# First layer's loop: TensorE's registers of adjacency slots and blocks are loaded one by one behind adjacency products, a pair of groups ahead

## What is computed

```python
# first layer, per edge
scores = jnp.sum(Q[tgt] * K[src], axis=-1) / math.sqrt(DK)
smax = jax.ops.segment_max(scores, tgt, num_segments=n)
sexp = jnp.exp(scores - smax[tgt])
...
# second layer, twice; the kernel does this sum as a product with a dense matrix
msg = x[src] * ew[:, None]
agg = jax.ops.segment_sum(msg, dst, num_segments=n)
...
x = _layernorm(x + layer(x), axis=-1)   # around each of the four
```

## Time and profile before

| | |
|---|---|
| Timed runs, median of 3 | 6169.95 us (6169.24 to 6170.06) |
| Profiled execution, span | 8199.2 us (the page gives no other time of it) |
| The loop in the profiled execution | 207 to 1930 us |
| TensorE busy in that stretch | 1252.18 us of 1723 |
| GpSimd busy in that stretch | 817.12 us |
| VectorE busy in that stretch | 914.52 us |
| ScalarE busy in that stretch | 611.39 us |
| Granted TensorE clock in that stretch | 0.71 of full speed |

### The profile page before, as it was taken

One profiled execution on the slowest core, in us unless ns is written; L12 is line 12 of the kernel. 1 busy time (PEld: TensorE's weight loads), 2 busy tenths in 40 slices (PEclk: granted clock), 3 DMA queues, 4 the chain that ended last, 5 costly groups with the idle time before them and its releaser, 6 DMA issues. The chain is left out here.

```text
span 8199.2 us, 128493 instructions
## 1 busy us (share of the span) xinstructions
PE 5007.5 (61%) x25366; PEld 3730.4 (45%) x25375; DVE 4287.8 (52%) x10883; ACT 2730.0 (33%) x6600; POOL 3533.6 (43%) x3882
## 2 busy tenths in 40 slices
PE   2677777774888935555556345555555355655557
PEld 2555555553664524444444334444444244444443
DVE  6555555556664145555555545554556445555554
ACT  1333333333542003333334323333334133333342
POOL 2544444442320044555554445555552555555520
PEclk7676677776999965555556556555556555555568
DMA  2444444443444722222222122222221222222215
GB/s 72 128 137 135 137 134 139 134 137 86 134 134 158 249 54 58 64 62 62 65 59 61 42 54 63 62 59 66 60 63 35 54 60 61 60 60 61 58 35 202
DMA packets 579250, 728.81 MB, mean 89 GB/s; under 512 B 90091, under 2 KB 424769, under 8 KB 578686
## 3 DMA queue, kind: packets, MB, share of 16 engines
q0 software_dynamic: 123968, 282.81, 14.9%
q1 hardware_dynamic: 304800, 350.53, 14.5%
q10 hardware_dynamic: 149918, 88.82, 4.0%
HBM read 601.07 MB, written 120.75 MB: 88 GB/s over the span
## 5 line engine op out<-in xcount | busy, mean ns | idle before, releaser
L1769 POOL DMA_INDIRECT rows<-scratch_gat,index x2496 | 2437.4, 977 | 2757.1 <-DVE mix L1997 1461.9
L2103 PE MATMUL sums<-xr_part,hot_t 128*128 x7524 | 1106.9, 283 | 786.2 <-issue 466.9
L2158 PE MATMUL sums<-mix,vhot 128*128 128x128 f32 x4992 | 1261.8, 421 | 91.0 <-issue 81.7
L2103 PEld LDWEIGHTS sums<-xr_part,hot_t 128*128 128x128 bf16 x7524 | 775.5, 121 | 1102.7 <-issue 945.7
L2011 DVE TENSOR_TENSOR z<-sums,rows 128x512 f32<-128x512 f32 x624 | 428.7, 687 | 1563.0 <-remote 1425.4
L1836 ACT ACTIVATE moved_sums<-sums x624 | 373.1, 598 | 2620.8 <-remote 1599.0
L932 POOL DMA_INDIRECT rows<-scratch_kv,index_ring x832 | 820.6, 986 | 887.5 <-ACT index_ring L1242 661.3
L2158 PEld LDWEIGHTS sums<-mix,vhot 128*128 128x128 f32 x4992 | 1044.4, 303 | 186.6 <-issue 142.6
L1368 PE MATMUL sums<-at_hot,lo_hot 128*128 128x200 f32 x2496 | 820.1, 493 | 16.4 <-issue 11.2
L1826 ACT ACTIVATE vhot<-iota,edge_local 128x128 f32<-128x128 f32 x2496 | 791.2, 392 | 0.1
L2154 PE MATMUL sums<-zeros 128*128 128x8 bf16 x624 | 114.7, 184 | 999.9 <-issue 551.5
(11 more groups left out here) (514 smaller groups left out, 6385.9 us busy)
## 6 DMA issues: line engine op xcount, KB each, us to landing
piece<-scratch_adj SPq DMA_DIRECT2D x90, 1280.0 KB, 6.3
local_ring<-scratch_local_rows SPq DMA_DIRECT2D x633, 128.0 KB
scratch_spool<-rows ACTq DMA_DIRECT2D x208, 256.0 KB, 2.6
vals<-scratch_spool SPq DMA_DIRECT2D x208, 256.0 KB, 2.6
scratch_adj<-stage SPq DMA_DIRECT2D x25, 1600.0 KB
rows<-scratch_gat,index POOLq DMA_INDIRECT x2496
local_ring<-scratch_local_rows ACTq DMA_DIRECT2D x211, 128.0 KB
mask<-scratch_masks SPq DMA_DIRECT2D x234, 80.1 KB
```

The costliest lines, as they stand in the source:

```text
L1769: eng.indirect_dma_start(rows[:, slot, q, k * LINE:(k + 1) * LINE], None, table, bass.IndirectOffsetOnAxis(ap=index[:, slot, s:s + 1], axis=0)
L2103: ins = eng.matmul(B.ps[:, at + k * D:at + (k + 1) * D], hot_t[:, slot, k * P:(k + 1) * P], part[:, bass.ds(at_block, D)], start=(j == 0), ...
L2158: ins = eng.matmul(B.ps[:, bass.ds(of_block * D, D)], hot[:, v % MIXES, k * P:(k + 1) * P], mix[:, v % MIXES, k * D:(k + 1) * D], start=Fa ...
```

## The change

The two loads at the head of each even group are taken out. In their place five loads of one register each stand behind adjacency products, and fill the registers of the next pair: three from `A.pe_table` behind the first three products of an even group, two from `B.blocks` behind the first two products of an odd group. The first pair's five loads stand ahead of the loop. Both tables get a pad of zeros for the pair behind the last. The registers are no longer handed over to the values read from them (`donate` is gone). On ScalarE, the value of the wait for room is worked out in a register of its own by two register instructions.

```diff
+    def fetch(self, at, n):
+        self.eng.load([self.regs[at]], self.B.blocks[0:1, bass.ds(n * GROUP, GROUP)].bitcast(I32))
+
+    def held(self, at):
+        return self.eng.snap(self.regs[at], min_val=0, max_val=(1 << 30) - 1)
...
-        self.pe_table = B.sb(ctx, "adj_pe_table", [1, A_STEPS], mybir.dt.uint8)
-        self.evac_table = B.sb(ctx, "adj_evac_table", [1, A_STEPS // 2], u16)
+        self.pe_table = B.sb(ctx, "adj_pe_table", [1, A_STEPS + A_TURN], mybir.dt.uint8)
+        self.evac_table = B.sb(ctx, "adj_evac_table", [1, (A_STEPS + A_TURN) // 2], u16)
...
+                eng.memset(A.pe_table[:, A_STEPS:], 0)
+                eng.memset(A.evac_table[:, A_STEPS // 2:], 0)
...
-                            need = field(twos[0], NEED_FIELD.bit_length() - 1, 32, BLOCKS - 1)
-                            eng.wait_ge(room.sem, need + (room.at(0) + 1))
+                            eng.reg_alu(need, twos[0] // NEED_FIELD, 31, ALU.bitwise_and)
+                            eng.wait_ge(room.sem, eng.snap(need, min_val=0, max_val=BLOCKS - 1) + (room.at(0) + 1))
...
+
+                def load_slots(pair, h, j):
+                    eng.load([regs[h][j]], A.pe_table[0:1, bass.ds(pair * A_TURN + 4 * j, 4)].bitcast(I32))
+
+                def load_ahead(i, q, k):
+                    h = q // 2 + 1
+                    if q % 2 == 0 and k < A_TURN // 4:
+                        load_slots(i * pairs + h, h % pairs, k)
+                    if q % 2 == 1 and k < 2:
+                        blocks.fetch(2 * (h % pairs) + k, i * RING_GROUPS + 2 * h + k)
+                for j in range(A_TURN // 4):
+                    load_slots(0, 0, j)
+                for k in range(2):
+                    blocks.fetch(k, k)
                 with eng.Fori(0, RING_TURNS) as i:
                     for q in range(RING_GROUPS):
                         n = i * RING_GROUPS + q
                         if q % 2 == 0:
-                            pair = i * (RING_GROUPS // 2) + q // 2
-                            eng.load(regs[q // 2], A.pe_table[0:1, bass.ds(pair * A_TURN, A_TURN)].bitcast(I32))
-                            slots = [eng.snap(r, donate=True, min_val=0, max_val=(1 << 31) - 1) for r in regs[q // 2]]
-                            fours = blocks.load(q, 2, n)
+                            slots = [eng.snap(r, min_val=0, max_val=(1 << 31) - 1) for r in regs[q // 2]]
+                            fours = [blocks.held(q), blocks.held(q + 1)]
...
                             if k % 2:
                                 ins.then_inc(summed.sem, 1)
+                            load_ahead(i, q, k)
```

More of the change, by code:

```diff
@@ L1104, in _ @@
                 slot(tmp, bank, 1)
-                link(eng.scalar_tensor_tensor(out=A.pe_table[:, :], in0=tmp[:, 0:A_STEPS], scalar=16.0, in1=read[:, 0:A_STEPS],
+                eng.memset(A.pe_table[:, A_STEPS:], 0)
+                eng.memset(A.evac_table[:, A_STEPS // 2:], 0)
+                link(eng.scalar_tensor_tensor(out=A.pe_table[:, 0:A_STEPS], in0=tmp[:, 0:A_STEPS], scalar=16.0, in1=read[:, 0:A_STEPS],
                                               op0=ALU.mult, op1=ALU.add))
@@ L1125, in _ @@
                     scalar=float(NEED_FIELD), in1=by_turn[:, :, 0], op0=ALU.mult, op1=ALU.add))
-                link(eng.tensor_copy(A.evac_table[:, :], read[:, 0:n]))
+                link(eng.tensor_copy(A.evac_table[:, 0:n], read[:, 0:n]))
                 next_block = bounds[0:1, 0:BLOCKS * BLOCK_WINDOWS].rearrange("p (k j) -> p k j", j=BLOCK_WINDOWS)[:, 1:BLOCKS, 0]
@@ L1261, in _ @@
                 regs = [[eng.alloc_register(f"evac{B.fresh()}") for j in range(A_TURN // 4)] for h in range(pairs)]
+                need = eng.alloc_register(f"need{B.fresh()}")
                 for n in range(3):
@@ L1295, in _ @@
                         keep(n, q)
-                for r in sum(regs, []):
+                for r in sum(regs, []) + [need]:
                     eng.free_register(r)
```

## The result

| | median of the runs, us | range, us |
|---|---|---|
| before | 6170.01 | 6169.24 to 6174.74 (4 runs) |
| changed | 6296.17 | 6292.02 to 6307.68 (4 runs) |

The ratio is 1.022, with a 95% interval from 1.0197 to 1.0242: slower by 126 us, 1.21 us for each of the 104 pairs. The prediction was slower by 35 us, and its range ended at 6250.

A forecast was written before the change was run, and what follows sets the result against it. TensorE's sequencer was taken as the bound. The middle of +27 and +80 us, 53, weighted by two thirds for low-clock groups, gave +35 us, the rest 0: 6170 to 6205, range 6090 to 6250.

The forecast's parts named there:

- What bounds the kernel: In the loop of 104 pairs, TensorE waits for its sequencer; without stalls a pair would be 10.65 us.
- everybody waits for TensorE: In the loop, GpSimd waits 651 us and ScalarE 581, TensorE only 31 for `hot_t`, so TensorE sets the pace.
- Removed and added: TensorE's sequencer loses a 1.70 us block at the pair's head and gains 2.47 us: 0.77 us more a pair.
- What hides it: Loads behind adjacency products: hidden at the low clock, lead of 0.5 us at the full clock; +35 us in all.
- the two views: Extra cost at the full clock: +0.26 us a pair (+27 us) seen from matmuls, +0.77 (+80 us) from the sequencer.
- What is late next: Adjacency sums come up to 1.5 us later, but ScalarE's 5.9 us before `hot_t` stays covered by TensorE's 6.2.
- The rest: Loads ahead of the loop, VectorE's clears and ScalarE's wait value: counted as 0, with +5 us for the range.
- Another engine sets the pace: Rival: GpSimd's 10.4 or ScalarE's 9.9 us a pair decides; within 12 us of 6170; no measurable change had 0.26.
- The loads get hidden: Rival: even group's three loads hidden at the low clock, 0.72 us a pair saved, 75 us, 6095; faster had 0.28.
- The change does not do what it says: Rival: loads don't overlap matmuls at either clock; 1.26 us a pair, +131 us, 6301; above 6250 had 0.04.
- What was to show it: Changed profile: 300 ns single loads, no 1.2 us even-head idle, full-clock adjacency parts 1.0 (even), 0.5 us (odd) longer.
- GpSimd's wait for index copies: Sign in the changed profile: if this wait grows instead of staying, the prediction's sum is wrong.

The follow-up runs named there:

- old loop: Loop of the kernel before with only ScalarE's edit of the change, profiled on a chip without the 0.7 us stalls; 6164.61 us against 6167.02.
- 2: Old loop with five single loads in place of the two bulk loads, all at the even group's head, nothing loaded ahead; 6217.17 us, ratio 1.0088.
- 5: Changed kernel with ScalarE's register load issued in the odd group before, behind `hot_t`; 6213.29 us, ratio 1.0077 to before.
- 6: Kernel before with ScalarE's register load issued in the odd group before, behind `hot_t`; 6152.86 us, ratio 0.9988.
- 3: Changed kernel with bulk loads in place of single ones, each behind a group's first product, a pair ahead; 6303.36 us, ratio 1.0232 to before.
- experiment 1: Kernel before with only ScalarE's edit of the change, the wait value worked out in its own register; 6164.61 us against 6167.02, ratio 1.0.
- 9: 6 with slots and blocks in one merged table, read by one load of five registers at the even head; 6139.95 us, ratio 0.9964 to before.
- 8: Changed kernel with only the three slot loads ahead in the even group, the block registers a bulk load at the pair's head; 6182.99 us, ratio 1.0033 to before.
- experiment 7: 3 with both bulk loads behind the even group's last product, at the odd group's head; 6256.41 us, ratio 1.015 to before.

## Why the prediction was wrong

The prediction left 0.04 to a time above 6250; 6296 was measured.

**What bounds the kernel: right where it was timed, but not read rightly.** On the timed chips TensorE's sequencer is at work for 11.06 of the old loop's 11.68 us a pair, and the loss lies in the loop only. That timed runs lack the 0.7 us stops was right too. But "TensorE waits 31 us for `hot_t`" was read from a view of idle matmul time. In the same trace of before the sequencer stood at that wait for 2.92 us in each pair, 304 us in all; 104 of these waits are over 1 us, and each ends 0.04 us behind the end of a `hot_t`. So the wait that later grew stood in the rows' trace already, and "everybody waits for TensorE" was half of it.

**Removed and added: right in kind, too small.** The sum was +0.77 us of sequencer time a pair; measured is +1.01 (12.07 less 11.06). The six new instructions with what lies between them were put at 0.56 (0.14 for addresses and six times 0.07) and came to 0.63. The loads were put at +0.20 (1.51 less 1.31) and came to +0.38 (2.35 less 1.97): 301 ns is the median of a single load in other loops, and the mean one is 470 ns here.

**What hides it: this step failed.** The prediction had the two views, +0.26 seen from the matmuls and +0.77 from the sequencer, took the middle, and gave it two thirds because loads at the low clock are hidden. The sequencer's view holds alone, and at both clocks. A lead hides an instruction only if the sequencer would have waited without it. Here it never waits except for `hot_t`: a lead that the low clock gives it is spent on the next group's scores. So the extra work counts in full, 1.01 times 104, 105 us, in place of 35, unless a wait takes it up: in 2 the old wait took up 0.36 of 0.87 us. The prediction had said this of the scores ("used up there anyway") and then averaged it away. The timeline shows it as well: the odd group's loads stand where the lead is nil, ahead of the low clock.

**What is late next: this one failed too.** "It stays covered, narrowly" set 5.9 us of ScalarE against 6.2 of TensorE. The wait was there before (0.62 us a pair) and grew to 0.96, 35 us. The 5.9 left out what ScalarE's chain hangs on: sums that come later and, in odd groups at the low clock, much later, and ScalarE's own register load, 1.18 us at the median and up to 3.2. 105 and 35 make the 140 us between the two profiles; they must, since work was defined as the rest, so they say where the time lies and not what each would cost alone. That the experiments say: with ScalarE's load ahead in both kernels (5 against 6) the change costs 60 us, with hardly any added work (3) a longer wait costs nearly all of 136, and moving ScalarE's one load takes 74 of the change's 126 away.

**The rest: right.** ScalarE's edit is worth 0 within what can be told (experiment 1).

**The rivals.** "Another engine sets the pace": GpSimd's eight gathers don't bind at 11.68 us a pair, since 9 runs at 11.35; where no load was added in the odd group (2, 8) the time moves with the sequencer's work, less what fills the old wait. "The loads get hidden" expected the low clock in the even group, where three loads would be free. It had moved to the odd group (0.49/0.09 became 0.15/0.61), and no load was free. The mean granted clock of the loop did not rise either (0.84 to 0.82). "The change does not do what it says" gave +131 us, close to the 126 measured, but its mechanism isn't seen: matmuls run on while a load is under way (four from 797.66 to 798.82 where loads began at 797.6), and the idle time behind one is 0.2 to 0.4 us. Its price is right because a load costs its whole time when the sequencer is the bound, whatever the matmuls do.

**What was to show it.** Single loads near 300 ns: yes for slots, 581 for blocks. No hole at the even head: yes. Adjacency parts at the full clock some 1.0 us longer in even groups: 1.5 us here, as 797.63 to 801.66 is 4.03 us, against 2.52 in the old loop's 803.15 to 805.67. GpSimd's wait for index copies, said to contradict the sum if it grew, did grow, 127.2 to 291.6 us, and that sign was right: the sum was wrong.

The Trainium skill ("Runtime: NRT & Kernel Launch", section "Instruction fetch mechanics") has the cost of a load per register, about 200 ns; it speaks of loads from HBM, and the tables here lie in SBUF. The rows have medians of 307 to 581 ns for one register, 545 for two and 990 for three: so the time does grow with the registers, but at 273 to 581 ns each.

## What to carry to other kernels

When an engine's sequencer hardly ever waits, its instructions are the pace: moving one behind a matmul hides nothing, and each that is added costs its full time, except for what an old wait takes up. See whether it waits in the sequencer's own records, since a view of idle matmul time charged 31 us where the sequencer stood for 304. Count its instructions, and use mean durations, not medians, where tails are long. Of two alternating groups, find the one whose results the other engines' chain starts from: a hole or an added load is cheap in the other one and dear in or ahead of this one, since what comes late there returns as a wait one turn later. And look for the slowest link of that chain on the other engine, here a register load that could be issued one turn earlier.

## What the runs showed of the hardware

- Register loads of TensorE's sequencer vary by what runs beside them: the same block load at the same place of the code takes 581 ns at the median in the changed kernel and 308 in experiment 5. The longer ones go with DMA traffic: of the changed kernel's slot loads, the half during which the 16 DMA engines were less busy has a median of 301 ns, the other half 552; for the old loop's loads of three registers it is 782 and 1274. One load of five registers took 584 ns at the least and 1276 at the median, less than the three- and two-register loads of the old loop together (990 and 545).
- ScalarE's load of its three registers took 1177 ns at the median at the pair's head (old loop) and 715 behind `hot_t` (experiment 5).
- Behind a group at the full clock, the next group's adjacency matmuls ran at 1.2 GHz for 0.27 of them where no idle time lay between, and for 0.96 where over 2 us did (eleven loops, table of experiment 7).
- The same kernel takes 6167 us on one chip and 8025 on another, where sequencer instructions at times last 0.7 us and ScalarE goes on 3.3 us behind the sum that it waited for; on the slower one the edit of experiment 3, which costs 2.3% elsewhere, is not seen.
